# Second attention of a hybrid block: three score banks and three shifted-score banks in turn by heads, one exponential per head

## What is computed

```
qkv = x @ qkv_w.T + qkv_b            # q, k, v: 16 heads of 8
q, k = rotary(q), rotary(k)
attn = softmax(einsum('abhqd,abhkd->abhqk', q, k) * hd ** -0.5)
out  = einsum('abhqk,bhkd->abhqd', attn, v)
out  = out.reshape(B, N, D) @ proj_w.T + proj_b
```

## Time and profile before

| | before |
|---|---|
| median of 3 runs | 1096.95 us (1095.75 to 1097.22) |
| profiled execution, its own time | 1095.75 us |
| its span, first to last instruction | 1094.0 us |
| busy: PE, DVE, ACT, POOL | 980.4, 968.9, 665.9, 365.1 us |
| mean granted clock of TensorE | 0.869 |

### The profile page before, as it was taken

The page is one execution under the profiler, slowest core; times in us unless marked ns, Lnnn a source line. Parts: engine busy times, 40 slices in busy tenths (PEclk is TensorE's granted clock), DMA queues, the critical chain, the costliest instruction groups (busy, mean ns, idle before and its releaser), DMA issues. The chain is left out here.

```text
span 1094.0 us, 17418 instructions
## 1 busy us (share of the span) xinstructions
PE 980.4 (90%) x5387; PEld 700.9 (64%) x5387; DVE 968.9 (89%) x1479; ACT 665.9 (61%) x776; POOL 365.1 (33%) x234
## 2 busy tenths in 40 slices
PE   7767887887569999999999899999879999999997
PEld 5533444444357888888887555455568888888886
DVE  7799999999987999999999787988689999999997
ACT  4779999999934454454454543666545445445444
POOL 2054666667802333333331210000204334334330
PEclk9855555555669999999999988999989999999999
DMA  2000000000128655555540000111149555555531
GB/s 58 1 1 1 1 1 1 1 1 1 51 55 195 167 152 148 157 152 147 157 135 0 1 1 1 23 21 14 34 96 215 158 155 145 156 155 146 154 84 38
DMA packets 50710, 86.93 MB, mean 79 GB/s; under 512 B 20092, under 2 KB 33404, under 8 KB 50556
## 3 DMA queue, kind: packets, MB, share of 16 engines
q1 hardware_dynamic: 50664, 86.34, 30.8%
HBM read 83.33 MB, written 2.98 MB: 79 GB/s over the span
## 5 line engine op out<-in xcount | busy, mean ns | idle before, releaser
L1493 ACT ACTIVATE sg<-ps 128x512 f32<-128x512 f32 x264 | 156.8, 594 | 265.0 <-PE ps L514 263.4
L514 PE MATMUL ps<-xh,whi 128*128 128x512 f32 x528 | 206.3, 391 | 1.3 <-ACT b L1319 1.3
L514 PE MATMUL ps<-xh,wlo 128*128 128x512 f32 x528 | 205.9, 390 | 0.0
L514 PE MATMUL ps<-xl,whi 128*128 128x512 f32 x528 | 205.8, 390 | 0.0
L2315 DVE TENSOR_TENSOR hf<-sg,ps 128x512 f32<-128x512 f32 x264 | 170.4, 684 | 31.1 <-DVE hl L2322 24.6
L1686 POOL CAST whi<-wraw 128x384 fp32r<-128x384 f32 x66 | 67.7, 1025 | 369.1 <-PE ps L514 284.8
L1626 POOL TENSOR_TENSOR rr<-xr,rr 128x2048 f32<-128x2048 f32 x32 | 145.3, 4571 | 124.5 <-ACT rr L1294 71.1
L2322 DVE TENSOR_TENSOR hl<-hf,hh 128x1024 fp32r<-128x1024 f32 x132 | 179.2, 1358 | 0.5 <-DVE hf L2315 0.5
L2327 DVE TENSOR_TENSOR hf<-hf,cbc 128x1024 f32<-128x1024 f32 x128 | 156.9, 1226 | 13.4
L1521 ACT ACTIVATE hh<-hf 128x1024 fp32r<-128x1024 f32 x132 | 139.2, 1054 | 4.3 <-DVE hf L2327 4.3
L1688 POOL TENSOR_TENSOR wlo<-wraw,whi 128x384 fp32r<-128x384 f32 x66 | 117.3, 1778 | 5.3
(11 more groups left out here) (277 smaller groups left out, 1537.5 us busy)
## 6 DMA issues: line engine op xcount, KB each, us to landing
cbc<-routing_coefficients SPq DMA_DIRECT2D x256, 256.0 KB, 3.9
wraw<-in_wexp_dram SPq DMA_DIRECT2D x66, 192.0 KB, 2.8
X<-in_x_dram SPq DMA_DIRECT2D x4, 256.0 KB, 4.7
routing_coefficients<-cT SPq DMA_DIRECT2D x8, 128.0 KB, 2.4
out_dram<-X SPq DMA_DIRECT2D x4, 256.0 KB, 2.9
heads_by_row<-o_all SPq DMA_DIRECT2D x12, 72.0 KB
b_rows<-heads_by_row SPq DMA_DIRECT2D x12, 72.0 KB, 2.7
rope_in<-in_consts_dram SPq DMA_DIRECT2D x1, 512.0 KB, 3.5
```

The costliest lines, as they stand in the source:

```text
L514: return pe.matmul(o, l, r, start=start, stop=stop, **kw)
L1493: act.activation(sg[c % 2][:, :], bank(4 + 2 * (c % 2)), ACT.Silu).then_inc(s_sg, 1)
```

## The change

Head h of the scores goes to bank h mod 3, and head h of the shifted scores to bank 3 + h mod 3. PE waits before the scores of head h for DVE's reading of head h - 3. Shifted scores of head h wait for the exponential of head h - 3: for the first head of unit U this is the last head of unit U - 2, as before; for the second head it is the first head of unit U - 1. PE signals every head of shifted scores by itself; ACT does two exponentials of 512 columns per unit, each with its own wait and signal. Counts of both semaphores are doubled where others wait for them, and the filler matmuls go to banks of the new scheme. The rest is as it was.

```diff
--- before.py
+++ after.py
@@ -381,6 +381,14 @@
 
             return 3 * (g % 2)
 
+        def score_bank(h):
+
+            return h % 3
+
+        def shifted_bank(h):
+
+            return 3 + h % 3
+
         def unit_b(U):
 
             G = U // UNITS
@@ -495,7 +503,7 @@
 
             load_second(1)
             sp.sem_inc(s_last, 1)
-            sp.wait_ge(s_s2, B * UNITS)
+            sp.wait_ge(s_s2, 2 * B * UNITS)
             sp.wait_ge(s_oTs, B + CHUNKS)
             first_coefs(1)
             sp.wait_ge(s_last, 5)
@@ -858,13 +866,13 @@
             def b_score_step(U, nt, i):
 
                 s, c, j0 = unit_b(U)
-                return mm(bank(i)[:, nt * N:(nt + 1) * N], b_qt[rows(j0 + i), c, tok(s, nt * P, P)],
+                return mm(bank(score_bank(2 * U + i))[:, nt * N:(nt + 1) * N], b_qt[rows(j0 + i), c, tok(s, nt * P, P)],
                           b_kt[rows(j0 + i), c, tok(s)], tile_position=(32 * (j0 + i), 0))
 
             def b_shifted_step(U, mt, i):
 
                 s, c, j0 = unit_b(U)
-                return mm(bank(2 + 2 * (U % 2) + i)[:, mt * N:(mt + 1) * N], b_kt[rows(j0 + i), c, tok(s, mt * P, P)],
+                return mm(bank(shifted_bank(2 * U + i))[:, mt * N:(mt + 1) * N], b_kt[rows(j0 + i), c, tok(s, mt * P, P)],
                           q2[U // UNITS % 2][rows(j0 + i), s % 4, :], tile_position=(32 * (j0 + i), 0))
 
             WAITS_FOR_PATH = {39: 4, 46: 3, 47: 4, 55: 4, 62: 3, 63: 4}
@@ -884,14 +892,16 @@
                 if shifted and U % (UNITS // 2) == 0:
                     pe.wait_ge(s_q2, U // (UNITS // 2) + 1)
                 if shifted and U >= 2:
-                    pe.wait_ge(s_e, U - 1)
+                    pe.wait_ge(s_e, 2 * U - 2)
                 if 0 <= U < 12:
-                    keep_busy(2 + 2 * (U % 2), 2)
+                    keep_busy(shifted_bank(2 * U), 2)
                 elif V in WAITS_FOR_PATH:
-                    keep_busy(2 + 2 * (U % 2), WAITS_FOR_PATH[V])
+                    keep_busy(shifted_bank(2 * U), WAITS_FOR_PATH[V])
                 for i in range(2):
-                    if scores and V >= 1:
-                        pe.wait_ge(s_mx, 2 * (V - 1) + i + 1)
+                    if scores and 2 * V + i >= 3:
+                        pe.wait_ge(s_mx, 2 * V + i - 2)
+                    if shifted and i == 1 and U >= 1:
+                        pe.wait_ge(s_e, 2 * U - 1)
                     for half in range(MT):
                         if scores:
                             last = b_score_step(V, half, i)
@@ -899,7 +909,7 @@
                                 last.then_inc(s_s1, 1)
                         if shifted:
                             last = b_shifted_step(U, half, i)
-                            if half == MT - 1 and i == 1:
+                            if half == MT - 1:
                                 last.then_inc(s_s2, 1)
 
             def b_max_transposed(s):
@@ -937,7 +947,7 @@
 
             def pv_b(C, half):
                 s, c, _ = unit_b(2 * C)
-                pe.wait_ge(s_e, 2 * (C + 1))
+                pe.wait_ge(s_e, 4 * (C + 1))
                 if C % 2 == 0 and half == 0 and C >= 2:
                     pe.wait_ge(s_bev, C // 2)
                 last = pv(vt, s, c, wr[:, C % CHUNKS, :], bank(6)[:, C % 2 * N:(C % 2 + 1) * N], (half,))
@@ -949,7 +959,7 @@
                     b_tiles(-1, V)
                     b_max_step(V)
                     if V >= AHEAD - 3:
-                        keep_busy(2, 6)
+                        keep_busy(3, 6)
                 for U in range(B * UNITS + 3):
                     V = U + AHEAD
                     b_tiles(U, V)
@@ -1387,11 +1397,12 @@
                 for U in range(B * UNITS + 3):
                     C = U // 2
                     if U < B * UNITS:
-                        act.wait_ge(s_s2, U + 1)
                         if C >= CHUNKS:
                             act.wait_ge(s_bpv, C - CHUNKS + 1)
-                        act.activation(wr[:, C % CHUNKS, U % 2 * UC:(U % 2 + 1) * UC], bank(2 + 2 * (U % 2), 2), ACT.Exp,
-                                       scale=SCALE_B).then_inc(s_e, 1)
+                        for h in (2 * U, 2 * U + 1):
+                            act.wait_ge(s_s2, h + 1)
+                            act.activation(wr[:, C % CHUNKS, h % 4 * MT * N:(h % 4 + 1) * MT * N], bank(shifted_bank(h)),
+                                           ACT.Exp, scale=SCALE_B).then_inc(s_e, 1)
                     if U >= 6 and U % 4 == 2:
                         copy_out((U - 6) // 4)
                     if U in (27, 43):
@@ -2176,7 +2187,7 @@
                     c, j0 = U % UNITS // 2, 2 * (U % 2)
                     for i in range(2):
                         dve.wait_ge(s_s1, 2 * U + i + 1)
-                        dve.tensor_reduce(mx[:, c, j0 + i, :], bank(i).rearrange("p (t m) -> p t m", t=MT),
+                        dve.tensor_reduce(mx[:, c, j0 + i, :], bank(score_bank(2 * U + i)).rearrange("p (t m) -> p t m", t=MT),
                                           AX_X, ALU.max).then_inc(s_mx, 1)
 
                 def max_split(s):
@@ -2203,7 +2214,7 @@
                 def shift(s, half):
                     dve.wait_ge(s_mq, 2 * s + half + 1)
                     if s >= 2:
-                        dve.wait_ge(s_s2, UNITS * (s - 1))
+                        dve.wait_ge(s_s2, 2 * UNITS * (s - 1))
                     cs = slice(2 * half, 2 * half + 2)
                     first, chunk, _ = unit_b(UNITS * s + 4 * half)
                     dve.tensor_tensor(q2[s % 2][:, cs, :], bank(7).rearrange("p (c n) -> p c n", c=2),
```

## The result

The changed kernel takes 1087.21 us (median of 5 runs, 1083.31 to 1090.63) against 1095.75 for the kernel before (5 runs, 1092.41 to 1097.22). The ratio is 0.9928, with a 95% interval of 0.9904 to 0.9953: it is faster by 0.7%, some 8 us. A second set (first experiment) gave 0.9926 (0.9903 to 0.995). Predicted were 1091.0 us against a median of 1096.95, 0.9946. The time of one kernel varies by 5 us and more between runs, so that ratios are taken within a set of runs, never between sets.

A forecast was written before the change was run, and what follows sets the result against it. DVE and PE, both near full, were taken to wait for each other in turn. Terms 4.6 - 1.2 + 1.6 + 1.2 - 0.2 = 6.0 us saved, against a median of 1096.95, gave 1091.0 us, range 1087 to 1096.

The forecast's parts named there:

- The third bank: Loop, V = 24 to 63: a third score bank removes DVE's idle time at listed places, 4.6 us saved.
- ACT's copy loop: Loop: exponentials at 1.05 us per unit delay the copy freeing bank 6; 0.3 us in four plain places, 1.2 us lost.
- The new wait of the second shifted head: PE's wait for the first exponential of unit U - 1: covered, taken as 0; bound 1.2 us for U < 12.
- U < 12: Steps where PE is the bound and keeps its fillers: the split between heads goes, 1.6 us saved.
- Lead-in: Twelve maxima of V = 2 to 7: PE writes while DVE reads, 1.2 us saved; bounds 0.6 and 3.
- Tail: Chain into DVE's routing: two short exponentials put off the copy, 0.2 us lost; bounds 0 and 1.0.
- rival A: Loop: DVE is never kept waiting, copies and path steps absorbed too; 10 us saved, 1087 us; chance 0.14.
- Rival B: PE stops at bank 6 or the new exponential wait instead; about 1 us saved, 1096 us; chance 0.15.
- Rival C: Loop: PE idles in one piece, its clock falls; 1110 us over all 40 steps, 1102 over half; chance 0.11.

The follow-up runs named there:

- first experiment: The changed kernel run once more with no edit, in a second set; 1087.92 us, ratio 0.9926 to the kernel before.
- score2: Changed kernel with two score banks in place of three; 1094.77 us, ratio 1.0002 to the kernel before.
- quarters: Changed kernel with each head's exponential cut into two of 256 columns; 1088.13 us, ratio 0.9923 to the kernel before.
- again: The changed kernel once more, no edit; 1087.92 us, ratio 0.9926 to the kernel before.
- nofill39: Changed kernel without the four fillers ahead of V = 39 and of V = 55; 1086.21 us, ratio 0.993 to the kernel before.
- shift2: Changed kernel with three score banks but only two shifted banks; 1093.42 us, ratio 0.9992 to the kernel before.
- fill0: Changed kernel without the two fillers ahead of each step for U < 12; 1086.39 us, ratio 0.9902 to the kernel before.
- fill0b: Changed kernel without the fillers for U < 12, run a second time; 1089.43 us, ratio 0.9947 to the kernel before.
- combo2: Changed kernel with one filler per step for U < 12 and none at V = 39, 46, 47, 55, 62, 63; 1098.83 us, ratio 0.9993.
- combo1b: Changed kernel with one filler for U < 12 and none at V = 39 and 55, second time; 1082.93 us, ratio 0.9887.
- old_less_fill: Kernel before, with one filler for U < 12 and none at V = 39 and 55; 1094.89 us, ratio 0.9978.

## Why the prediction was right, point by point

- **The third bank, 4.6 us for V = 24 to 63.** Right, and it is the whole effect (score2). The places came out as argued: plain steps without idle but for 0.32 in one round, nothing left of the waits ahead of first shifts, V = 47 and 63 gone, V = 44 and 60 at 0.48 where half of 0.9 was taken, V = 39 and 55 unchanged at 0.97. Measured over the stretch: 73.03 - 68.66 = 4.4 us.
- **ACT's copy loop, 1.2 us taken back.** This term was too large by 1.0. With all places together the stretch became 4.4 us shorter where 4.6 were counted, so 0.2 is left for it. Of the four plain places that were charged with 0.3 one shows in the trace: the 0.32 of DVE behind PE's wait of 0.46 for the copy. Adding some more to ACT in quarters cost the loop 0.3. The pair of exponentials has 0.96 us from its start to the next instruction, not 1.05 (0.48 for each, where the spacing behind a copy, 0.52, was taken). That DVE's reserve of up to a head did the rest is likely, but no run tests it.
- **The new wait of the second shifted head, 0.** It does appear, 3.3 us in nine places, but on PE, beside DVE's work. That it is cheap depends on the third shifted bank: with two, 5.5 us of the gain are gone at the median.
- **U < 12, 1.6 us.** 22.48 - 20.85 = 1.6.
- **Lead-in, 1.2 us.** The maxima up to the split are 1.4 us shorter, 7.26 us for twelve where 8.63 stood. What follows varies from 8.6 to 10.5 us with the moment at which the clock rises: +0.5 us in the first trace, where it rises at about 662, and -1.0 in `again`, at about 660. I had this as a bound, not as scatter that every run has.

```profile
648.16 7.26 DVE L2190 TENSOR_REDUCE mx<-ps 128x2 f32<-128x512 f32 x12 [0.18 <-PE ps L522]
```

- **Tail, -0.2 us.** 11.94 - 11.73 = 0.2. In the kernel of quarters 12.20.
- **The sum.** Without the stretch behind the split the terms measured are 4.4 + 1.6 + 1.4 - 0.2 = 7.2 us, with it 6.7 and 8.2 in two traces; the runs say 7.9 (0.72% of 1095.75). Forecast were 6.0, short of the 7.2 by 1.0 of the ACT term and 0.2 of the lead-in. The 0.7 between 7.2 and 7.9 is within the scatter.
- **The number, and luck.** The ratio forecast, 0.9946, lies inside the measured interval. The time itself, 1087.21 us, lies outside the 1088.5 to 1094 that had a chance of 0.60, and only 0.2 us inside the range, at the end that was put there for rival A, whose mechanism did not occur. The kernel before also came out 1.2 us lower with two more runs, 1095.75 against the 1096.95 that the forecast started from. So the mechanism and most terms were right; that the time fell just inside and not just outside is luck.
- **Rival A** (10 us, DVE never waits) fell on V = 39 and 55, which stayed, as argued, and where the fillers, not the banks, hold PE (nofill39). **Rival B** (the wait moves to bank 6 or the exponentials): it moved, but beside the path. With two shifted banks it comes close: in the trace of shift2 weight loads wait 10.1 us for exponentials in the loop and DVE 4.8 us for PE. **Rival C** (the clock falls): not in the changed kernel, whose two traces have 1.00 throughout the loop. Its point and price were near: fill0, at 0.50 for 49 us, has a stage 10.4 us longer than fill0b. The cause I named did not appear: PE is busy 64.41 of 68.60 us in the loop, 0.94 as before and not 0.8. Its busy time and the stretch both became some 4 us shorter. What I left out is that C's chance hangs on the fillers, which the change keeps. The page's rule on cycling through banks ("A second HAM failure mode: psum-queue depth-cycling" in the Trainium skill's "TensorE: Matmul & The Clock Gate") is not borne out by the cycling as such: the changed kernel cycles one head at a time at 1.00. Its short idle gaps between groups of matmuls do stand ahead of the falls in shift2 and combo2. But combo1b fell with no gap in the 6 us before, and the changed kernel has PE idle for 0.76 of the 2 us from 708 and stays at 1.00, so gaps alone don't tell when it falls.

## What to carry to other kernels

Where two engines hand a buffer back and forth and are both 90% busy or more, as here, try one more buffer on the side that waits. Here the gain could be counted beforehand place by place from the slower engine's starts, not from its idle totals. Where banks are fixed in number, halve the unit of work on the side that has time to spare, and check that it keeps as many buffers as it needs: with one shifted bank fewer the gain was gone at the median. Leave filler work that keeps the matmul clock up in place when a change shortens waits, and take it away only where a trace shows that it delays the bound, with enough runs to see the clock fall in one of them.

## What was not expected of the hardware

- The same program, without fillers for U < 12, ran the loop at granted clock 0.50 for 49 us in one trace and was back at 1.00 after some 10 us in another. While it was low, PE was busy for 48.67 of 49.00 us by the profile, mostly with tiles of 32 rows or 32 columns of the array, and still the clock did not rise. It rose at about 719 us, behind four fillers that use the whole array (first line). In combo2 at about 750 and in old_less_fill at about 728 it rose behind eight projection matmuls over the whole array (the second line is combo2's). But in fill0b it was back with neither ahead of it, so three cases suggest what raises it and don't show it.

```profile
716.29 2.06 PE L522 MATMUL ps<-sel 128*128 128x512 f32 x4
```

```profile
747.58 2.08 PE L522 MATMUL ps<-wo_b,b_oT 128*128 128x128 f32 x8
```

- Leaving out work can cost more than it saves by a wide margin: the fillers of V = 46, 47, 62 and 63, on which DVE never waited in the changed kernel, were worth about 16 us at the median where the others are left out or halved (combo2, 1098.83, against combo1b, 1082.93, in one set).
- Cutting one exponential of 1024 columns into two of 512 costs ACT 0.04 us, 0.96 against 0.92 us from its start to the next instruction.
